# Linear attention: the denominators behind the first value product, the next input pair made at the first chunk, the last feed-forward's weight pieces on ScalarE

## What is computed

```
q, k = elu(x W_Q') + 1, elu(x W_K') + 1      # 8 heads of 64
v    = x W_V'
S_t  = g S_(t-1) + k_t v_t'                   # g = sigmoid(decay_log), one per head
z_t  = g z_(t-1) + k_t
y_t  = (S_t' q_t) / (z_t . q_t + 1e-6) * sigmoid(x W_g' + b)
out  = y W_O'
```

## Time and profile before

| | |
|---|---|
| median of 3 runs | 1887.92 us (1887.57 to 1888.78) |
| profiled execution | 1887.85 us, span 1886.0 us |
| TensorE busy | 1843.9 us, 98% of the span |
| VectorE busy | 1395.0 us, 74% |
| ScalarE busy | 881.7 us, 47% |
| GpSimd busy | 589.6 us, 31% |
| linear attention | from about 815 us to 1612 us of the span |
| mean granted TensorE clock | 0.999 of full speed |

### The profile page before, as it was taken

The page is one execution under the profiler, slowest core; times in us unless marked ns, Lnnn a source line. Parts: engine busy times, 40 slices in busy tenths (PEclk is TensorE's granted clock), DMA queues, the critical chain, the costliest instruction groups (busy, mean ns, idle before and its releaser), DMA issues.

```text
span 1886.0 us, 36455 instructions
## 1 busy us (share of the span) xinstructions
PE 1843.9 (98%) x12481; PEld 1541.7 (82%) x12481; DVE 1395.0 (74%) x2679; ACT 881.7 (47%) x1717; POOL 589.6 (31%) x526
## 2 busy tenths in 40 slices
PE   8999999999999999999999999999999998999998
PEld 7888888888888888878787888788878877888887
DVE  6566566556668888777777878787878788888885
ACT  6656656665554444453333333333333332444443
POOL 5313203311332222233433333333333334522211
PEclk9999999999999999999999999999999999999999
DMA  7100000000022122120000000000000001222322
GB/s 246 43 1 0 0 0 0 0 0 0 13 54 54 29 33 32 29 62 13 13 12 12 11 11 11 11 11 11 11 11 11 12 12 20 38 62 62 65 55 58
DMA packets 230630, 53.19 MB, mean 28 GB/s; under 512 B 209696, under 2 KB 228768, under 8 KB 230176
## 3 DMA queue, kind: packets, MB, share of 16 engines
q1 hardware_dynamic: 229296, 49.53, 13.0%
q10 hardware_dynamic: 1264, 2.76, 0.4%
HBM read 18.69 MB, written 8.39 MB: 14 GB/s over the span
## 4 chain that ended last, share of the span: by engine, by line
PE 74%; DVE 9%; issue 6%; POOL 4%; SPq 2%; ACT 2%; DMA 1%; DVEq 0%; ACTq 0%; POOLq 0%
PE PS L1203 16%; PE PS L1212 9%; PE PS L322 8%; PE PS L331 7%; PE PS L861 7%; PE PS L832 6%; PE PS L850 3%; PE PS L1732 3%; PE PS L1706 3%; PE PS L1668 3%; SPq L270 2%; PE PS L1711 2%; PE PS L1721 2%; PE PS L872 2%; DVE lin_zq L1504 2%
## 5 line engine op out<-in xcount | busy, mean ns | idle before, releaser
L322 PE MATMUL PS<-ln_xh,lin_w 128*128 128x512 f32 x768 | 249.9, 394 | 9.2 <-POOL ln_xl L280 5.4
L1135 ACT ACTIVATE ff_silu<-PS 128x512 f32<-128x512 f32 x192 | 114.4, 597 | 232.9 <-PE PS L1203 204.5
L1170 DVE SCALAR_TENSOR_TENSOR ff_h<-PS,ff_silu 128x512 f32<-128x512 f32 x192 | 131.2, 684 | 107.7 <-PE PS L1203 94.1
L322 PEld LDWEIGHTS PS<-ln_xh,lin_w 128*128 128x128 f32 x768 | 144.3, 188 | 47.6 <-DVE lin_kT L1487 8.6
L568 POOL TENSOR_TENSOR qk<-qk,swapped 64x128 f32<-64x128 f32 (+2 forms) x96 | 96.9, 1009 | 240.2 <-DVE swapped L712 234.4
L1154 DVE TENSOR_TENSOR ff_h_lo<-ff_h,ff_h_hi 128x512 fp32r<-128x512 f32 x192 | 165.1, 860 | 0.4
L861 PE MATMUL PS<-probT,v_a 128*128 128x128 f32 x1152 | 153.3, 278 | 0.0
L861 PEld LDWEIGHTS PS<-probT,v_a 128*128 128x128 f32 x1152 | 139.5, 192 | 14.3 <-ACT probT L632 7.4
L322 PE MATMUL PS<-ln_xl,lin_w 128*128 128x512 f32 x384 | 150.2, 391 | 0.0
L832 PE MATMUL PS<-qk 128*128 128x512 f32 (+3 forms) x384 | 145.2, 489 | 1.0 <-POOL qk L568 0.9
L722 DVE TENSOR_REDUCE neg_max<-PS 128x1 f32<-128x256 f32 (+7 forms) x128 | 95.6, 752 | 62.3 <-PE PS L835 60.9
(11 more groups left out here) (190 smaller groups left out, 5354.2 us busy)
## 6 DMA issues: line engine op xcount, KB each, us to landing
ff_raw<-ln_xn SPq DMA_DIRECT2D x464, 32.0 KB, 2.0
ln_xl<-ln_xn SPq DMA_DIRECT2D x288, 32.0 KB, 2.0
out_x<-X SPq DMA_DIRECT2D x15, 512.0 KB, 2.9
X<-in_x SPq DMA_DIRECT2D x7, 1024.0 KB, 5.5
stage<-in_w_lin SPq DMA_DIRECT2D x1, 2048.0 KB, 8.1
stage<-in_w_gate SPq DMA_DIRECT2D x2, 768.0 KB, 7.4
stage<-in_w_up SPq DMA_DIRECT2D x2, 768.0 KB, 8.8
stage<-in_w_down SPq DMA_DIRECT2D x2, 768.0 KB, 10.2
```

The lines of the kernel that those rows point to most:

```text
L322: last = nc.tensor.matmul(out, w, x, start=n == 0, stop=n == len(terms) - 1)
L1135: nc.scalar.activation(silu[:, f % NB_GU, :], PS[:, f % NB_GU, :], ACT.Silu, scale=W_SCALE).then_inc(silu_done.sem, 1)
L1170: nc.vector.scalar_tensor_tensor(h[:, f % 2, :], PS[:, NB_GU + f % NB_GU, :], W_SCALE, silu[:, f % NB_GU, :], ALU.mult, ALU.mult).then_inc ...
```

## The change

Four things change, all in the linear attention's programs. TensorE does `denominators` after item 12 (the first value product) instead of after item 11. VectorE does `sums_by_query` of pairs 0 and 1 at items 5 and 7 instead of 4 and 6. ScalarE does `act_high` ahead of all chunks, and GpSimd does `pool_low` at c = 0 instead of c = 2. In the last half `ff2_high` goes from GpSimd to ScalarE, ahead of `gated_high` of chunks 0, 1 and 2, and GpSimd's last two calls change places.

```diff
@@ GpSimd, turn
                         if c > 0:
                             gated_low(b, UT * half + c - 1)
-                        if c == 2:
+                        if c == 0:
                             nfront.pool_low(pool, n, 0)
-                        if last and half == NHALF - 1 and c < 2:
-                            ff2_high(c)
-                        if last and half == NHALF - 1 and c == 3:
-                            ff2_high(2)
                     if first and half == NHALF - 1:
                         ff_float()
                 if last:
+                    gated_low(b, TB - 1)
                     following.ln.pool_rstd(pool, 2)
-                    gated_low(b, TB - 1)
@@ ff2_high, from GpSimd's program to ScalarE's
-                    nc.gpsimd.tensor_copy(env["ff2_w_hi"][:, piece], stage[:, piece]).then_inc(ff2_signals.prep_hi, 1)
+                    nc.scalar.activation(env["ff2_w_hi"][:, piece], stage[:, piece], ACT.Copy).then_inc(ff2_signals.prep_hi, 1)
@@ ScalarE, turn
+                    nfront, n = next_of(b, half, last)
+                    nfront.act_high(act, n, 0)
                     for c in range(UT - 1):
+                        if last and half == NHALF - 1:
+                            ff2_high(c)
                         gated_high(b, UT * half + c)
-                        if c == 0:
-                            nfront, n = next_of(b, half, last)
-                            nfront.act_high(act, n, 0)
@@ VectorE, turn
                         if it in (3, 5):
                             key_sums(b, half, it // 2 - 1)
-                        elif it in (4, 6):
-                            sums_by_query(b, half, it // 2 - 2)
-                        elif it == 2 * NP - 1:
+                        if it == 5:
+                            sums_by_query(b, half, 0)
+                        if it == 2 * NP - 1:
+                            sums_by_query(b, half, 1)
                             for j in range(NP // 2, NP):
                                 key_sums(b, half, j)
@@ TensorE, turn
                             keys(b, half, 0)
+                        if it == 3 * NP:
                             if first and half == 0:
                                 pe.wait_ge(zeroed, 5)
                             denominators(b, half)
```

More of the change, by code:

```diff
@@ L1437, in decay_tables, with ff2_high @@
                 last.then_inc(decays, 1)
+            def ff2_high(n):
+                if n == 0:
+                    act.wait_ge(proj_ready.sem, proj_ready.at(NB - 1, NHALF * NITEM))
+                    act.wait_ge(env["ff_float"], 1)
+                part = (slice(0, KT * FF), slice(KT * FF, 2 * KT * FF), slice(2 * KT * FF, NW))[n]
+                for at in range(part.start, part.stop, M):
+                    piece = slice(at, at + M)
+                    nc.scalar.activation(env["ff2_w_hi"][:, piece], stage[:, piece], ACT.Copy).then_inc(ff2_signals.prep_hi, 1)
             def gated_high(b, ch):
```

## The result

The changed kernel takes 2034.51 us (median of 4 runs, 2033.31 to 2036.67), the kernel before 1888.35 us beside it: a ratio of 1.0773, 95% interval 1.0760 to 1.0787, or 146 us slower. The forecast was 2031 us. The profiled execution has a span of 2031.5 us, 145.5 more than before.

The account below looks back on a forecast made before the run. TensorE, busy 98% of the span, was taken as the bound. Later halves of 116 us plus 27 us of halved clock, 143 us on the profiled 1887.85 us, gave 2031 us, range 2000 to 2058.

Parts of the forecast that it names:

- What bounds, and what sets the landing: TensorE, busy 98%, bounds; SyncE's 16 issues at 0.611 us plus 2.0 us make the pair land 11.8 us after VectorE's blocks.
- The low part in front of the decay: On GpSimd, chunk 1's decay waits behind the low part; L1711 comes 7.28 us later in second halves; 116 us in all.
- 0.3 us back: In second halves, denominators behind item 12 move VectorE's inverse and the blocks 0.3 us later.
- 0.2 us back: In first halves, denominators behind item 12 make VectorE's work 0.2 us later.
- VectorE's two products one item later: Same VectorE instructions reordered, ending before item 12: taken as 0, bounds -0.4 and +0.4 us a half.
- The clock: TensorE's clock halves behind each of 16 stops, losing 1.7 us each, 27 us in all; ends 0 and 54 us.
- The rival in which it doesn't fall: TensorE's clock stays up or is back in time after the stops: 2004 us; chance 17%.
- The sum: 116 us of later halves plus 27 us of clock, 143 us on the profiled 1887.85 us: 2031 us.
- what would show it: Expected profile signs: L1711 waits 16 times for 7 to 8 us, a half takes 55 to 58 us, mean clock drops.
- The very first half: TensorE's wait of 3.44 us there shrinks by 1.42, but the pair is not earlier.
- The edits at nothing: Last half's weight pieces on ScalarE: 0, or up to 4 us; swap of GpSimd's last calls: 0, within 2.
- The faster rival: If the pair lands by 1191.5, before chunk 1's decay on GpSimd, the moves win their waits: 1874 us; chance 2%.

Follow-up runs that it names:

- e6b: The changed kernel with 8 of the pair's 16 transfers issued by ScalarE instead of SyncE: 1946.11 us, ratio 1.0302 to the kernel before.
- e11: The kernel before with only GpSimd's low part moved to c = 0: 2039.61 us, ratio 1.0796.
- e8b: The kernel before with only VectorE's two products one item later: 1887.87 us, ratio 0.9995.
- e5b: The changed kernel with 6 long float32 matmuls, results unused, ahead of TensorE's wait for the state of chunk 2: 2018.38 us.
- e9: The kernel before with only TensorE's denominators behind the first value product: 1885.68 us, ratio 0.9984.
- e10: The kernel before with only the last half's weight pieces on ScalarE and GpSimd's last two calls swapped: 1889.17 us, ratio 1.0002.
- e7b: The changed kernel with the high part back behind chunk 0's gated_high, low part at c = 1, transfers issued from two queues: 1875.02 us.
- e3: The kernel before with only ScalarE's high part ahead of the chunks, low part still at c = 2: 1954.70 us, ratio 1.0340.
- e4: The changed kernel with 52 short matmuls, results unused, per half ahead of TensorE's wait for the state of chunk 2: 2044.47 us.

## Why the prediction was right

**What bounds, and what sets the landing: right.** All 16 high parts start at the landing, and the landing follows the issue. e6b shows it by moving it.

**The low part in front of the decay: right, and shown alone by e11.** From the low part's start to L1709 the forecast had 1205.56 - 1201.26 = 4.30 us; measured 1271.96 - 1267.67 = 4.29. The sum had 116 us net of the waits that go. TensorE's time without work rises by 111.2 us, so this term was 5 us too large.

**The landing: off in both directions.** "0.3 us back" in second halves was 0.5 (42.6 against 42.1). "0.2 us back" in first halves was 0.6 us forward (42.1 against 42.7). The step that failed is "VectorE's two products one item later ... I take 0". Before, one of them ran into GpSimd's `qsT` product in the first halves and took 1.82 us; the order alone, in e8b, brings the landing to 42.0.

**The clock: right in kind, 27 us was too small.** The Trainium skill (TensorE: Matmul & The Clock Gate, Part 1) has the clock halved behind idleness and given back after sustained work. The rows of the changed kernel agree (0.50 behind each of the 16 stops, then 1.00). TensorE's matmuls take 34.3 us more, 2.1 a stop instead of 1.7, because the half speed lasted 3.5 to 6.1 us after a restart, in most of them about 5 or 6, not the 3.4 us of the earlier trace rows. The rival in which it doesn't fall is refuted by the granted clock, and e5b wins 16 us by keeping TensorE busy.

**The sum: in part luck.** It had 116 + 27 = 143 us; measured in the profiled span, 111.2 + 34.3 = 145.5. That it is off by 2.5 us only comes of two errors of opposite sign, 5 us too much for the stops and 7 too little for the clock. A half takes 57.5 or 58.5 us, where the forecast of what would show it said 55 to 58.

**The very first half.** Its wait of 3.44 us shrank to 2.55, so by 0.9 and not by 1.42, and the clock there no longer falls. The denominators' place alone (e9) brings it to 2.1, VectorE's order alone (e8b) to 3.9: once more the order is not nothing.

**The edits at nothing.** The weight pieces and the swap: right, e10 can't be told from the kernel before. As the stop of 2.25 us in the last half shrinks, other waits there grow.

**The faster rival's condition was not tested to its end.** It asked for a landing by 1191.5, 8 us earlier. e6b gets 4.9 of them and still loses 57 us, which fits; no run has the rest. The way found to use an earlier pair was to keep the decay of chunk 1 in front: e7b.

## What to carry to other kernels

Before a step is moved up in an engine's program, look at what it waits for: if that arrives late, everything that it is moved past is late with it, and here one moved call of 2.4 us cost 16 stops of 8 us because it stood in front of a 1 us link of a recurrence. Move the arrival first (here, issue the transfers from two queues), then the call, and only as far as the gap in which it fits. A stop of TensorE can cost more than its length (here 2.1 us more for each of 8.1), so a sum of waits has to have a term for the slow matmuls behind each.

## What the runs showed of the hardware beyond that

TensorE's granted clock fell to 1.2 GHz in or behind stops of 7.7 to 9.3 us in the changed kernel, of 3.44 us before, of up to 4.3 us in e3, and in e5b's second halves behind one of 2.35 us. It stayed at 1.00 behind 2.68 us in most of e5b's first halves, behind 3.60 us in e3's fourth half, and behind the last half's 2.25, 1.97 and 1.91 us in the kernel before, while a stop of 1.91 us in e3, at 1675 us, was followed by a fall. So the length of the stop alone doesn't tell.

VectorE's product of two SBUF tensors (L1513) took 1.82 us beside GpSimd's `qsT` product in seven of the eight first halves of the kernel before, where GpSimd's had begun 0.01 to 0.02 us ahead of it, and 0.91 us in e8b, one item later. In six of these halves the product ahead of it began 0.05 us before GpSimd's and took 0.69 us; there GpSimd's took 1.79 us instead of 1.29. In these rows the one that began second was the slow one.

And 832 more matmuls on TensorE (e4) cost more than the clock that they kept: five waits of about 2.2 us with no releaser, and a later landing of another engine's transfers.
